# A fused two-layer attention kernel: another way to start the first pass, ffn products in column tiles, and another slot table

## The chip, the cores and the metric

The kernel runs on one core of one Trainium2 chip. The metric is device time in microseconds. The text names the engines as the profile does: PE (matrix products, with PEld for its weight loads), DVE (vector), ACT (activations), POOL, and SP, which only issues transfers.

## The reference, cut to what matters

The input is x, 4 sequences of 1024 tokens with 128 channels. Two layers follow, each an attention and a feed-forward part with a residual and a layernorm behind each. What concerns this case is the first attention and the first feed-forward part:

```python
qkv = einsum('bnc,fc->bnf', x, qkv_w); q, k, v = split(qkv, 3)
q = l2norm(q); k = l2norm(k)             # over all 128 channels of a row
# 16 heads of 8 channels; q and k each times 8**-0.5
attn = softmax(q @ k.T / temperature)    # all 1024 keys
x = layernorm(x + (attn @ v) @ proj_w.T + proj_b)
# ffn of layer 0: int8 product, x quantised row by row
x = layernorm(x + (round(x / scale) @ weight_q.T) * scale * weight_scale + bias)
```

Layer 1 has causal attention with a layernorm and rope on q and k of each head, and a gated silu feed-forward part.

## The kernel before

Tokens are taken in 8 chunks of 512 (`NCH`). One *pass* is one group of 4 heads for 512 queries of one sequence in one layer; there are 64 passes (`PASSES`), taken in pairs. In layer 0 a pass goes over 8 key tiles of 128 keys, in two halves: the first pair of passes takes key tiles 0 to 3 of pass 0, 0 to 3 of pass 1, then 4 to 7 of pass 0 and 4 to 7 of pass 1 (`pair_steps`). A *step* is one key tile (or a packed pair of tiles) for 4 heads. There are 400 steps, and each gives two exps (numbered k = 2s and 2s + 1) of 128x1024, the 800 ACTIVATEs of line 717. For exp k PE makes the scores (`scores`, L874) into one of three PSUM slots, ACT writes `probs`, and PE adds probs times v into bank ACC (`sums`, L896). `scores(k)` waits until exp k - 3 is done.

**Parts and rows.** PE multiplies in a reduced float32 format. To keep precision, q and k are each split into a rounded high part and the rest, the low part (`prep_part`, `mid_part`). A head's 32 rows of `q_st` and `k_st` hold its 8 channels four times (`PRODUCTS`): high and low of q against high and low of k. The rows are laid out by DMA: for most passes through a scratch tensor in DRAM, for pass 0 and the first keys of pass 1 straight from the part tiles (`first_rows`, one DMA for each product y).

**The side work.** All that prepares later passes and finishes earlier ones (qkv products, norms, transposes, layernorms, ffn, gate and up) is cut into units and put between the steps by a table written out beforehand, `ORDER`: one word for each step, whose letters take the next unit of a lane (p: chunk preparation for layer 0, m: middle part, l: last part, c: constants, t: turning the sums). `<` puts the side work ahead of the sums of that slot, `|` puts the sums between the two scores. PE units write the one bank SIDE, DVE reads it, and `side_read` hands it back.

**The head.** Ahead of the steps PE runs 10 dummy bf16 products (`keep_warm`, L930), then the qkv products of chunks 0 and 1 (L938, 128x384 each, into 8 banks). ACT squares q and k of both chunks (L689), copies v and the chunk 1 rows (L703). DVE works out the flags that pick the program's branch, the inverse roots of chunk 0 (9 small operations, L1103 to L271), scales k and q (L1117); PE transposes both (L752); DVE and ACT make the parts (L1332, L1333, L700, L1336). SP and ACT then issue 8 DMAs for pass 0's rows, SP 8 more for pass 1's. PE fills the time with 22 dummy products, takes the branch, and starts `scores`. POOL makes constants; the large memset of `v_st` is behind its first copies.

Of the kernel before, what the change touches and what calls it, by code (L numbers as in the profile page):

```python
# [6 lines left out]
ALU = mybir.AluOpType  # L7
# [132 lines left out]
FIRST_KEYS = [("prep", 1, "pe", "qkT", 1), ("prep", 1, "dve", "scale_q", 0), ("prep", 1, "pe", "qkT", 0)]  # L140
# [17 lines left out]
p p p - - - - <pc < <p - p < <cpp <pp - <t c <p <pp  # L158
- <pc < <p < <p - <p - <ppp < p |t |t |tppmm m - |mmm |p <m
p < mm mmm <mm mmm | |m tm < <m < <m < <mmm - mp <mmm - mp  # L160
m <pm m - |t <tm tm mm <p mm m m pm mmp <mm <mm |m |mmpp |m <
ptm - <m < <m < <m < mmmp <m mp mm pm m p m <tt <m tm <m
<mpm < <mmp <m <mp mmpp <m <mm mmm mp | |m tmp - m - m - <m mm
mm pm - <pm mp < mmp - |t <m tt m m mtp |m <p |mm m <t <mt
tm ll mml <mmm m <m |mml |m pmp m plm mm m <l t <l <mlmm l mp |l
ml ml <m m - l <mp l <l <ll lt <p t <t llmm <pmm mpm - mmp <
lp m m |t <mm mmp <mm <m p m <p <mpp <m <mp <m m <mtt <mm |m |tm
m p <m mp ll <mll m - ll < <l < |tl l l l - |l < l
- l < l < <llll l l |t | |tt mm m <t m mm <mm | |tmm |
|ttl l <lm <m |mm <mml mml m < m m mmm - l t mlm lm ml m |l  # L170
ml ml < <m l l l <ll <l <lm tt < tm <m <m |mm |m |mm |m mm
- |mmlmm | |tmm | |m m < m < m <l <m m m <m |tm | |tmtlm -
<m <ll mm ml < m < ll - <l | <l tl - | |l l l - <l
- <l < <l < <l <ll <l |lltt | |tm mm < t m < <mmm m |ttm |m
<tl <mmm - |mmm |ml |lm lm lm m m ml tlm |l ml lm l l l <mmlm l
<lm m llm < |tt <ml tll < l |t - <llll - l tl tl <tm <lm <mlm <l
<l l <l <lm <llll ml - <lmt <m <m m m m m m m <mm < - mm
mmt
# [95 lines left out]
def program(nc, a, ctx):  # L274
# [11 lines left out]
    w_cols = sb("w_cols", [P, 6 * C + 4], F32)  # L286
    w_qkv = [w_cols[:, 0:3 * C], w_cols[:, 3 * C + 4:6 * C + 4]]
    tcol = w_cols[:, 3 * C:3 * C + 1]
# [51 lines left out]
    job["prep"]["sq"] = job["prep"]["qk"]  # L340
    job["mid"]["sq"] = tok["mid"]["both"][:].rearrange("p a t c -> p (a t c)").rearrange("p (t c) -> p t c", t=TC)
# [16 lines left out]
    head_bank = {1: ps[:, TC, :], 0: ps[:, TC + 1, :]}  # L358
# [13 lines left out]
    more_rows_in, second_rows_in = sem("more_rows_in"), sem("second_rows_in")  # L372
# [9 lines left out]
    tcol_made, head_high = sem("tcol_made"), sem("head_high")  # L382
# [22 lines left out]
    WARM = (10, 4, 0, 22, 7)  # L405
# [15 lines left out]
    def first_rows(eng, p, u, dst, y):  # L421

        part = job["prep"]["part"][p * HR:(p + 1) * HR, u, y % PARTS if u else y // PARTS, :]
        eng.dma_start(dst[y:P:PRODUCTS, p, 0:HALF].bitcast(F32), part.bitcast(F32)).then_inc(rows_in[p], 16)
# [32 lines left out]
    def _(sp):  # L457
# [34 lines left out]
        load_x(1)  # L492
        for dst, src in ((w_qkv[1], a["w1_qkv"]),
# [10 lines left out]
        for u, dst in ((1, k_st), (0, q_st)):  # L504
            sp.wait_ge(parts_ready, 2 - u)
            for y in range(PRODUCTS // 2):
                first_rows(sp, 0, u, dst, y)
        for u, dst in ((1, k_st), (0, q_st)):
            for y in range(PRODUCTS):
                first_rows(sp, 1, u, dst, y)  # L510
# [67 lines left out]
    def _(pool):  # L578
# [67 lines left out]
        send_parts(pool, "prep", 1, 1)  # L646
# [5 lines left out]
        todo = [(s + 1, 0, "mask", s) for s in range(NS) if STEPS[s][3]]  # L652
# [9 lines left out]
        for _, _, what, n in todo:  # L662
            if what == "bias":
                add_bias(n)
            elif what == "mask":
                mask(n)
            elif what == "load":
                load_v(n)
            else:
                store_v(what, n)  # L670
# [3 lines left out]
    def _(act):  # L674
# [4 lines left out]
        def head():  # L679

            act.dma_start(w_cols[:, 0:3 * C + 1], a["w0_qkv"]).then_inc(w_in, 16)
            act.dma_start(small[:], a["small"].partition_broadcast(P)).then_inc(small_in, 16)

            def square(c, t):
                for u in range(2):
                    done = 2 * (c * TC + t) + u
                    if done:
                        act.wait_ge(norms_ready, done)
                    nc.scalar.activation(squares, ps[:, c * TC + t, u * C:(u + 1) * C], ACT.Square,  # L689
# [715 lines left out]
```

## Time and profile before

| | us |
|---|---|
| median of three runs | 810.7 (809.85 to 811.05) |
| the profiled execution | 810.68 |
| its span, first to last instruction | 808.6 |
| PE busy | 791.6 |
| ACT busy | 767.8 |
| DVE busy | 527.7 |
| POOL busy | 174.7 |

Times in views count from the span's start. The profiled execution took 2.08 us more than its span. A busy PE isn't a PE at its peak, since ends of pipelined matmuls are modelled.

### The profile page before, as it was taken

How to read it: one execution, taken by the hardware profiler on the slowest of the kernel's cores; microseconds unless marked ns; L12 is line 12 of the kernel's file. 1: busy time of each engine (PE TensorE's matmuls, PEld its weight loads, DVE VectorE, ACT ScalarE, POOL GpSimd, SP SyncE). 2: the span in 40 equal slices, each digit the busy share in tenths (PEclk: the TensorE clock that was granted, in tenths of full speed). 3: DMA queues.
4: the chain of work that ended last, by engine and by line, in shares of the span. 5: the costliest groups of instructions: out<-in, count | busy, mean ns of one | idle time of the engine just before them, and what ended most of it. 6: DMA issues, size and time to landing. Idle time of an engine off the chain costs nothing.

```text
span 808.6 us, 18428 instructions
## 1 busy us (share of the span) xinstructions
PE 791.6 (98%) x7469; PEld 295.9 (37%) x7469; DVE 527.7 (65%) x1422; ACT 767.8 (95%) x869; POOL 174.7 (22%) x370
## 2 busy tenths in 40 slices
PE   8999999999999999999999999999999999999996
PEld 4333333333333433443333433343333343443444
DVE  4253657758758788687862685766573387787646
ACT  4999999999999999999999999999999999999982
POOL 3111101101102601033100511023300263363220
PEclk9999999999999999999999999999999999999999
DMA  5776232415404711532170431231231231053000
GB/s 148 253 235 208 89 122 82 154 41 183 144 28 157 272 41 40 183 144 93 41 260 27 124 112 42 92 128 44 92 131 51 69 130 54 28 182 120 15 15 16
DMA packets 48553, 88.71 MB, mean 110 GB/s; under 512 B 5200, under 2 KB 14544, under 8 KB 48464
## 3 DMA queue, kind: packets, MB, share of 16 engines
q1 hardware_dynamic: 47696, 85.95, 31.2%
q8 instruction: 61, 1.00, 0.5%
q0 software_dynamic: 288, 1.05, 0.4%
q10 hardware_dynamic: 480, 0.48, 0.2%
q14 instruction: 28, 0.23, 0.1%
HBM read 50.50 MB, written 35.65 MB: 107 GB/s over the span
## 4 chain that ended last, share of the span: by engine, by line
PE 74%; ACT 14%; DVE 7%; issue 3%; POOL 1%; DMA 0%; ACTq 0%; DVEq 0%; POOLq 0%
PE ps L896 36%; PE ps L874 21%; ACT probs L717 13%; PE ps L763 8%; PE ps L752 3%; PE ps L849 2%; DVE th L1282 1%; DVE hT L1283 1%; PE ps L930 1%; PE ps L757 1%; ACT th L677 0%; PE ps L938 0%; DVE gate_sb L1279 0%; POOL v_all L590 0%; PE ps L791 0%
## 5 line engine op out<-in xcount | busy, mean ns | idle before, releaser
L717 ACT ACTIVATE probs<-ps 128x1024 f32<-128x1024 f32 x800 | 745.9, 1057 | 15.3 <-PE ps L874 11.3
L896 PE MATMUL ps<-probs,v_st 128*32 128x512 f32 (+3 forms) x3584 | 425.0, 556 | 3.3 <-issue 1.8
L874 PE MATMUL ps<-q_st,k_st 32*128 32x512 f32 (+3 forms) x1792 | 257.4, 459 | 2.1 <-ACT probs L717 0.9
L874 PEld LDWEIGHTS ps<-q_st,k_st 32*128 32x128 f32 x1792 | 119.6, 182 | 281.8 <-ACT probs L717 226.5
L627 POOL TENSOR_SCALAR_AFFINE_SELECT probs<-probs 128x256 f32<-128x256 f32 x256 | 104.3, 430 | 141.0 <-ACT probs L717 138.9
L896 PEld LDWEIGHTS ps<-probs,v_st 128*32 128x32 f32 x3584 | 79.9, 108 | 110.2 <-issue 80.9
L595 POOL COPY v_st<-v_all 128x256 f32<-128x256 f32 (+1 forms) x65 | 25.6, 402 | 343.3 <-PE ps L896 335.2
L1256 DVE COPY mid_qkv<-ps 128x384 f32<-128x384 f32 x32 | 17.8, 558 | 45.5 <-PE ps L763 43.8
L1137 DVE STREAM_TRANSPOSE sums_t<-ps 128x512 f32<-128x512 f32 x32 | 22.9, 717 | 29.1 <-PE ps L896 29.0
L1287 DVE TENSOR_TENSOR last_y<-ps,last_y 128x128 f32<-128x128 f32 x24 | 7.0, 292 | 42.6 <-PE ps L763 42.6
L849 PE MATMUL ps<-yTp,w_hid 128*128 128x512 f32 x84 | 30.8, 448 | 1.7 <-DVE gate_sb L1279 0.3
L1256 DVE COPY prep_qkv<-ps 128x384 f32<-128x384 f32 x24 | 13.4, 557 | 27.4 <-PE ps L763 27.0
L590 POOL COPY v_all<-mid_qkv 128x512 f32<-128x512 f32 x9 | 14.0, 1552 | 66.4 <-DVE mid_qkv L1256 61.5
L763 PE MATMUL ps<-w_cols,yT 128*32 128x384 f32 x256 | 26.8, 491 | 0.0
L763 PE MATMUL ps<-w_down,hT 128*32 128x128 f32 x672 | 23.9, 275 | 0.6 <-DVE last_y L1287 0.3
L1233 DVE TENSOR_TENSOR x_all<-ps,x_all 128x512 f32<-128x512 f32 x15 | 10.4, 692 | 20.5 <-PE ps L763 19.3
L1282 DVE SCALAR_TENSOR_TENSOR th<-th,gate_sb 128x512 f32<-128x512 f32 x21 | 14.7, 698 | 13.5 <-PE ps L849 10.8
L1279 DVE COPY gate_sb<-ps 128x512 f32<-128x512 f32 x21 | 14.5, 691 | 13.1 <-PE ps L849 12.8
L763 PEld LDWEIGHTS ps<-w_down,hT 128*32 128x32 f32 x672 | 17.9, 110 | 12.2 <-issue 6.8
L849 PEld LDWEIGHTS ps<-yTp,w_hid 128*128 128x128 f32 x84 | 12.5, 188 | 24.8 <-DVE gate_sb L1279 10.3
L617 POOL TENSOR_TENSOR x_all<-x_all,vecs 128x512 f32<-128x512 f32 x16 | 20.4, 1278 | 0.6 <-DMA x_all<-in_x 0.6
L763 PE MATMUL ps<-w_cols,xT 128*32 128x384 f32 x192 | 20.2, 492 | 0.0
(192 smaller groups left out, 636.2 us busy)
## 6 DMA issues: line engine op xcount, KB each, us to landing
k_st<-parts_scratch SPq DMA_DIRECT2D x46, 512.0 KB, 3.5
parts_scratch<-mid_part SPq DMA_DIRECT2D x34, 512.0 KB, 4.0
q_st<-parts_scratch SPq DMA_DIRECT2D x62, 256.0 KB, 3.9
parts_scratch<-prep_part SPq DMA_DIRECT2D x28, 512.0 KB, 4.3
k_st<-parts_scratch SPq DMA_DIRECT2D x17, 256.0 KB, 2.8
xT<-in_xT SPq DMA_DIRECT2D x8, 256.0 KB, 4.2
x_all<-in_x SPq DMA_DIRECT2D x8, 256.0 KB, 6.6
out<-yo SPq DMA_DIRECT2D x7, 256.0 KB, 2.3
```

The costliest lines, as they stand in the source:

```text
L595: return g_.tensor_copy(v_st[:, p % VB, t, :, p % 2 * SR:p % 2 * SR + D], v_all[:, layer, b % 2, t, g * GH * D:(g + 1) * GH * D] .rearrang ...
L617: g_.tensor_tensor(x_all[:, c, :, :], x_all[:, c, :, :], bc(vecs[:, 3 * layer, :].unsqueeze(1), [P, TC, C]), ALU.add).then_inc(bias_added, 1)
L627: op = g_.affine_select(out=block_, in_=block_, compare_op=ALU.is_ge, fill=0.0, base=0, pattern=[[0, 2], [1, P]], channel_multiplier=-1)
L717: nc.scalar.activation(probs[:, k % PS, :, 0:w], slot(k)[:, :, 0:w], ACT.Exp).then_inc(probs_ready, 1)
L752: last_ = tp(dst[:, t * P:(t + 1) * P], src(t), idn[:])
L763: last_ = mm(dst[row, :], src[:, row], w, start=first, stop=last)
L849: last_ = mm(side, w_hid[:, 0 if what == "gate" else 1, k * P:(k + 1) * P], yTp[:, n, :], start=(n == 0), stop=(n == PARTS - 1))
L874: last_ = mm(slot(k)[:, e, at:at + n], k_st[row, p % KB, kt * P:(kt + 1) * P], q_st[row, p % KB, lo:HALF], start=True, stop=not shifted)
L896: last_ = mm(acc[HR * h:HR * (h + 1), lo:HALF], v_st[:, p % VB, kt, h, :], probs[:, (2 * s + h // 2) % PS, h % 2, at:at + n], start=FIRST[ ...
L1137: v.transpose(sums_t[:], acc).then_inc(sums_turned, 1)
L1256: v.tensor_copy(job[name]["qkv"][:, k, :], side[:, 0:3 * C]).then_inc(side_read, 1)
L1282: chain[lane(name, c)].link(stt(out=th[:, k % 2, :], in0=th[:, k % 2, :], scalar=1.0, in1=gate_sb[:, k % 2, :], op0=ALU.add, op1=ALU.mult))
```

## The change

- **Pass 0's rows in place.** Chunk 0's products are made as q, k and v groups of 4 products of 128x128 in banks ACC, SIDE and 5. DVE takes k's squares with `bn_stats`. It writes the scaled q and k of the first 4 heads with every channel four times over (`first_qk`), so that PE's transpose gives all 128 rows at once. ACT writes them times +1 or -1 by row, rounded, and DVE adds the unrounded rows times 0 or 1, which gives high or low part by row. No DMA is in this. The second keys of pass 0 come the same way from chunk 1, as a unit `firstT` in slot 3.
- **The usual parts of chunk 0** (`head_turn`) are made behind the first three `scores`. SP and POOL then load the rows of pass 1, each DMA as soon as its part is there, and SP stores the parts to DRAM right behind; sums of step 0 wait for these parts. The DRAM load of pass 1's second keys is replaced by 4 DMAs from the part tile. Four DMAs that ACT issued are gone, and four of pass 0's second keys.
- **Dummy products**: 8 instead of 10, then 3, then 8 (instead of 4 and 22), and two each behind scores 4, 5 and 7 instead of scores 3 to 6.
- **POOL** does its memsets ahead of the v copies; its store of chunk 1's k parts moves into its list.
- **SP** holds the 9 loads of later constants until x's first chunk has landed.
- **ffn**: four products of 32 output columns in place of each 128x128 one.
- **ORDER** is another table. The same units, plus `firstT` and `scale_k`, in the same order within each lane.

```diff
-FIRST_KEYS = [("prep", 1, "pe", "qkT", 1), ("prep", 1, "dve", "scale_q", 0), ("prep", 1, "pe", "qkT", 0)]
+FIRST_KEYS = [("prep", 1, "pe", "firstT", 1), ("prep", 1, "dve", "scale_k", 0), ("prep", 1, "pe", "qkT", 1), ("prep", 1, "dve", "scale_q", 0), ("prep", 1, "pe", "qkT", 0)]
...
-p p p - - - - <pc < <p - p < <cpp <pp - <t c <p <pp
...
+- - | <pc ppc p p - <p p < <p - <pp <p <p <tp p < p
...
-    WARM = (10, 4, 0, 22, 7)
+    HEAD_SQUARES = 2
+    WARM = (8, 3, 8, (4, 5, 7))
...
+        eng.dma_start(dst[y:P:PRODUCTS, p, 0:HALF].bitcast(F32), part.bitcast(F32)).then_inc(done or rows_in[p], 16)
...
+        sp.wait_ge(x_in[0], 16)
...
+            for low in range(PARTS - u):
+                sp.wait_ge(*((parts_ready, 2 - u) if low else (head_high, 2 - u)))
+                for y in range(PRODUCTS):
+                    if (y % PARTS if u else y // PARTS) == low:
+                        first_rows(sp, 1, u, dst, y)
+        store_parts("prep", 0, 1)
+        store_parts("prep", 0, 0)
...
+            sp.dma_start(k_st[y:P:PRODUCTS, 1, HALF:S].bitcast(F32),
+                         job["mid"]["part"][HR:2 * HR, 1, y % PARTS, :].bitcast(F32)).then_inc(second_rows_in, 16)
...
+        pool.wait_ge(qkv_copied, 1)
+        pool.sem_inc(v_stored["prep"], 1)
+        pool.wait_ge(pool_consts, POOL_CONSTS + 1)
+        copy_v(0, slice(0, TC)).then_inc(v_in, 1)
+        store_v("prep", 1)
+        pool.wait_ge(v_stored["prep"], 2)
+        copy_v(0, slice(TC, KT)).then_inc(more_v_in, 1)
+        pool.wait_ge(parts_ready, 1)
+        for y in range(1, PRODUCTS, PARTS):
+            first_rows(pool, 1, 1, k_st, y, low_rows_in)
...
+        todo = [(slot_of("prep", 1, "qkT", 1) + 1, 0, "send", 1)] + [(s + 1, 0, "mask", s) for s in range(NS) if STEPS[s][3]]
...
+                send_parts(pool, "prep", n, 1)
...
+            act.wait_ge(head_qkv, 1)
             for t in range(TC):
-                act.wait_ge(head_qkv, t + 1)
...
+                square(t, ps[:, ACC, t * P:(t + 1) * P], job["prep"]["st"][:, 0, 2 * t:2 * t + 1])
+            act.wait_ge(head_qkv, 3)
+            nc.scalar.activation(v_all[:, 0, 0, tiles_of(0), :], ps[:, V_BANK, :].rearrange("p (t c) -> p t c", t=TC),
+                                 ACT.Copy).then_inc(qkv_copied, 1)
...
-                if t == TC - 1:
+                act.wait_ge(head_qkv, 4 + t)
+                for u in range(2 if t < HEAD_SQUARES else 0):
+                    square(TC + 2 * t + u, ps[:, t, u * C:(u + 1) * C], job["mid"]["st"][:, 0, 2 * t + u:2 * t + u + 1])
+                if t == HEAD_SQUARES:
...
+                    for u in (1, 0):
+                        act.wait_ge(first_turned, 2 - u)
+                        nc.scalar.activation(first_sign[:, u, :], ps[:, FIRST_BANK[u], :], ACT.Copy,
+                                             scale=(sign_q, sign_k)[u]).then_inc(first_signed, 1)
+                nc.scalar.activation(job["mid"]["qkv"][:, t, :], ps[:, t, 0:3 * C], ACT.Copy).then_inc(
+                    qkv_copied if t == TC - 1 else head_copied, 1)
...
-                pe.wait_ge(side_read, fill)
+            pe.wait_ge(*((side_read, fill) if fill else (parts_ready, 2)))
...
-                    last_ = mm(side[:, t * P:(t + 1) * P], xqT[:, t * P:(t + 1) * P], w_ffn[:], start=True, stop=True)
+                    last_ = quarters(side[:, t * P:(t + 1) * P], xqT[:, t * P:(t + 1) * P], w_ffn[:])
...
+            elif what == "firstT":
+                pe.wait_ge(first_scaled, 3)
+                last_ = turn4(lambda t: first_qk[:, t, k, :, :].rearrange("p f y -> p (f y)"), side, ident)
...
-                    pe.wait_ge(rows_in[p % KB], 32 * (p // KB + 1) + (32 * PRODUCTS - 32 if p % KB < 2 else 0))
+                    pe.wait_ge(*((first_made, 2) if not p else (rows_in[p % KB], 32 * (p // KB + 1) + {0: -32, 1: 32 * PRODUCTS - 64}.get(p % KB, 0))))
+                    if p == 1:
+                        pe.wait_ge(low_rows_in, 16 * PARTS)
...
-                pe.wait_ge(more_rows_in, 16 * PRODUCTS)
+                pe.wait_ge(side_read, FILL["prep", 1, "firstT", 1] + 1)
             if k % 2 == 0 and tiles_[0][0:2] == (1, TC):
-                pe.wait_ge(second_rows_in, 16)
+                pe.wait_ge(second_rows_in, 16 * PRODUCTS)
...
+                pe.wait_ge(parts_ready, 2)
...
-        keep_warm(WARM[0], SIDE)
+        keep_warm(WARM[0], 0)
...
+        pe.wait_ge(x_in[0], 16)
+        for n, bank in enumerate((ACC, SIDE, V_BANK)):
             for t in range(TC):
-                mm(ps[:, c * TC + t, 0:3 * C], xT[:, c, t * P:(t + 1) * P], w_qkv[0],
-                   start=True, stop=True).then_inc(head_qkv, 1)
+                last_ = mm(ps[:, bank, t * P:(t + 1) * P], xT[:, 0, t * P:(t + 1) * P], w_qkv[0][:, n * C:(n + 1) * C],
+                           start=True, stop=True)
+            last_.then_inc(head_qkv, 1)
+        pe.wait_ge(x_in[1], 16)
+        for t in range(TC):
+            mm(ps[:, t, 0:3 * C], xT[:, 1, t * P:(t + 1) * P], w_qkv[0], start=True, stop=True).then_inc(head_qkv, 1)
+        keep_warm(WARM[1], FIRST_BANK[1])
...
+        pe.wait_ge(qkv_copied, 1)
...
+            pe.wait_ge(first_scaled, 2 - u)
+            for t in range(TC):
+                last_ = tp(ps[:, FIRST_BANK[u], t * P:(t + 1) * P], first_qk[:, t, u, :, :].rearrange("p f y -> p (f y)"), ident[:])
+            last_.then_inc(first_turned, 1)
+        pe.wait_ge(head_copied, 1)
+        keep_warm(WARM[2], 0)
...
+        pe.wait_ge(qkv_copied, 2)
...
+        def head_turn(u):
+            pe.wait_ge(qk_ready["prep"], 2 - u)
+            turn4(lambda t: job["prep"]["qk"][:, t, u * C:(u + 1) * C], ps[:, ACC + u, :], ident).then_inc(head_turned, 1)
...
+                head_turn(1)
+                head_turn(0)
...
+                    if k in WARM[3]:
+                        pe.wait_ge(parts_ready, 1)
+                        keep_warm(2, SIDE)
...
-                        keep_warm(2, ACC)
...
+            if not part:
+                ch.step(v.tensor_reduce(m[:, 0:1], temp, AX.X, ALU.max, apply_absolute_value=True))
+                ch.step(v.tensor_reduce(m[:, 2:4], gb[:, 0, :, :], AX.X, ALU.max, apply_absolute_value=True))
+                return
+            ch.need()
+            ch.step(ts(far[:, 0:1], m[:, 0:1], BOUND * D, None, ALU.is_gt))
...
+            elif what == "firstT":
+                chain[name].link(ts(first_sign[:, k, :], side, sign_k, None, ALU.mult))
+                stt(out=k_st[:, 0, HALF:S], in0=side, scalar=low_k, in1=first_sign[:, k, :].bitcast(F32),
+                    op0=ALU.mult, op1=ALU.add).then_inc(side_read, 1)
...
+        def head():
+            ch, part, qk = chain["prep"], job["prep"]["part"], job["prep"]["qk"]
+            per = lambda c, k: buffers("prep", c)["st"][:, k, 0:2 * TC].rearrange("p (t u) -> p t u", u=2)
+            by_t = lambda x: x.rearrange("p (t c) -> p t c", t=TC)
+            roots = lambda c: [rows_norm("prep", c, what) for what in ("rs1", "rs2")]
+            dve.wait_ge(head_qkv, 2)
+            bn, mv, mean2 = tok["last"]["bn"], tok["last"]["st"][:, 0, :], tok["last"]["st"][:, 1, 0:TC]
+            mean, var = mv[:, 0:2 * TC:2], mv[:, 1:2 * TC:2]
+            for t in range(TC):
+                ch.step(v.bn_stats(bn[:, t, :], by_t(side)[:, t, :]))
+            ch.need()
+            for t in range(TC):
+                ch.step(v.bn_aggr(mv[:, 2 * t:2 * t + 2], bn[:, t, :]))
+            ch.need()
+            ch.link(stt(out=mean2, in0=mean, scalar=float(C), in1=mean, op0=ALU.mult, op1=ALU.mult))
+            ch.link(stt(out=per(0, 0)[:, :, 1], in0=var, scalar=float(C), in1=mean2, op0=ALU.mult, op1=ALU.add))
+            dve.wait_ge(norms_ready, TC)
+            roots(0)
+            for u in (1, 0):
+                op = tt(first_qk[:, :, u, :, :], by_t(ps[:, ACC + u, :])[:, :, 0:HR].unsqueeze(3).to_broadcast([P, TC, HR, PRODUCTS]),
+                        per(0, 1)[:, :, u].unsqueeze(2).unsqueeze(3).to_broadcast([P, TC, HR, PRODUCTS]), ALU.mult)
+                op.then_inc(first_scaled, 1)
+            flags(1)
+            for u, dst in ((1, k_st[:, 0, 0:HALF]), (0, q_st[:, 0, :])):
+                dve.wait_ge(first_signed, 2 - u)
+                stt(out=dst, in0=ps[:, FIRST_BANK[u], :], scalar=(low_q, low_k)[u], in1=first_sign[:, u, :].bitcast(F32),
+                    op0=ALU.mult, op1=ALU.add).then_inc(first_made, 1)
+            for u in (1, 0):
+                tt(qk[:, :, u * C:(u + 1) * C], by_t(ps[:, ACC + u, :]), bc(per(0, 1)[:, :, u].unsqueeze(2), [P, TC, C]),
+                   ALU.mult).then_inc(qk_ready["prep"], 1)
+            dve.wait_ge(head_turned, 1)
+            v.tensor_copy(part[:, 1, 0, :], side).then_inc(head_high, 1)
+            dve.wait_ge(head_high, 1)
+            tt(part[:, 1, 1, :], side, part[:, 1, 0, :].bitcast(F32), ALU.subtract).then_inc(parts_ready, 1)
+            dve.wait_ge(head_turned, 2)
+            ts(part[:, 0, 0, :], acc, tcol, None, ALU.mult).then_inc(head_high, 1)
+            dve.wait_ge(head_high, 2)
+            stt(out=part[:, 0, 1, :], in0=acc, scalar=tcol, in1=part[:, 0, 0, :].bitcast(F32), op0=ALU.mult,
+                op1=ALU.subtract).then_inc(parts_ready, 1)
+            dve.wait_ge(qkv_copied, 2)
+            late = slice(HEAD_SQUARES, TC)
+            wide = lambda x: x.rearrange("p t (u c) -> p t u c", u=2)
+            rest = job["mid"]["sq"][:, late, :]
+            ch.link(tt(rest, job["mid"]["qkv"][:, late, 0:2 * C], job["mid"]["qkv"][:, late, 0:2 * C], ALU.mult))
+            ch.link(v.tensor_reduce(per(1, 0)[:, late, :], wide(rest), AX.X, ALU.add))
+            dve.wait_ge(norms_ready, TC + 2 * HEAD_SQUARES)
+            roots(1)
+            tt(first_qk[:, :, 1, :, :], job["mid"]["qkv"][:, :, C:C + HR].unsqueeze(3).to_broadcast([P, TC, HR, PRODUCTS]),
+               per(1, 1)[:, :, 1].unsqueeze(2).unsqueeze(3).to_broadcast([P, TC, HR, PRODUCTS]), ALU.mult).then_inc(first_scaled, 1)
...
+        flags(0)
+        head()
...
+def low_and_sign():
+    y = np.arange(P) % PRODUCTS
+    low = np.stack([y // PARTS, y % PARTS]).astype(np.float32)
+    return np.stack([low[0], 1 - 2 * low[0], low[1], 1 - 2 * low[1]], axis=1)
```

## Rows read from the trace of the kernel before

**Rows 1.** The page: busy time by engine, and the chain that ended last

```profile
PE 791.6 (98%) x7469; PEld 295.9 (37%) x7469; DVE 527.7 (65%) x1422; ACT 767.8 (95%) x869; POOL 174.7 (22%) x370
...
PE 74%; ACT 14%; DVE 7%; issue 3%; POOL 1%; DMA 0%; ACTq 0%; DVEq 0%; POOLq 0%
```

**Rows 2.** Timeline of ACT, 19 to 790 us: start, length, count, idle before

```profile
19.83 126.84 ACT L717 ACTIVATE probs<-ps 128x1024 f32<-128x1024 f32 x137 [4.08 <-PE ps L874]
```

**Rows 3.** Waits of ACT, 40 to 784 us: total, times, longest

```profile
ACT probs L717 <- PE ps L874: 7.2, 27, 0.6
```

**Rows 4.** Timeline of all engines, 0 to 14 us

```profile
1.27 4.45 PE L930 MATMUL ps<-warm 128*128 128x512 bf16 x10 [1.27 <-DVE warm L997]
...
5.08 0.77 PEld L938 LDWEIGHTS ps<-w_cols,xT 128*128 128x128 f32 x2 [0.28 <-DMA w_cols<-in_w_qkv]
...
5.51 5.63 PE L938 MATMUL ps<-w_cols,xT 128*128 128x384 f32 x16
...
10.04 0.17 DVE L1103 TENSOR_SCALAR prep_st<-prep_st 128x8 f32<-128x8 f32 x1 [1.55 <-ACT attn L689]
...
11.05 0.48 ACT L703 ACTIVATE mid_qkv<-ps 128x384 f32<-128x384 f32 x1
...
11.87 1.29 DVE L1117 TENSOR_TENSOR prep_qk<-ps,prep_st 128x512 f32<-128x512 f32 x2
...
12.61 1.32 PE L752 MATMUL ps<-ident,prep_qk 128*128 128x128 f32 x8
```

**Rows 5.** Timeline of all engines, 14 to 32 us (a merged row may start earlier)

```profile
13.76 4.91 PE L930 MATMUL ps<-warm 128*128 128x512 bf16 x22
...
14.03 0.69 ACT L700 ACTIVATE prep_part<-ps,w_cols 128x512 fp32r<-128x512 f32 x1 [0.42 <-PE ps L752]
...
14.88 0.75 DVE L1336 SCALAR_TENSOR_TENSOR prep_part<-ps,w_cols,prep_part 128x512 fp32r<-128x512 f32 x1 [0.16 <-DVE prep_part L1333]
...
19.30 0.73 PE L874 MATMUL ps<-q_st,k_st 32*128 32x512 f32 x6 [0.63 <-DMA q_st<-prep_part]
...
19.83 13.19 ACT L717 ACTIVATE probs<-ps 128x1024 f32<-128x1024 f32 x14 [4.08 <-PE ps L874]
...
19.88 2.51 SPq L424 DMA_DIRECT2D q_st<-prep_part  x4
```

**Rows 6.** Line 938 alone, 0 to 12 us: ns min/median/max

```profile
L938 PEld LDWEIGHTS ps<-w_cols,xT x16: 190/190/338, 5.1 to 10.3; 128*128 128x128 f32 x16
L938 PE MATMUL ps<-w_cols,xT x16: 485/487/794, 5.5 to 10.7; 128*128 128x384 f32 x16
```

**Rows 7.** Timeline of the kernel's end: small f32 products, bn_stats and bn_aggr

```profile
786.92 1.16 PE L777 MATMUL ps<-x_all,ident 128*128 128x128 f32 x8
...
789.74 0.97 DVE L1190 BATCH_NORM_STATS2 last_bn<-ps 128x6 f32<-128x128 f32 x4 [0.32 <-PE ps L783]
...
790.75 0.38 DVE L1065 BATCH_NORM_AGGREGATE last_tok<-last_bn 128x2 f32<-128x6 f32 x4
```

**Rows 8.** The DMAs of line 424, from issue to landing

```profile
DMA to landing us min/median/max: 2.1/2.1/2.3
```

**Rows 9.** Line 449: how long POOL takes to issue a DMA, ns

```profile
L449 POOL DMA_DIRECT2D parts_scratch<-mid_part x2: 786/793/800, 22.4 to 23.1; - x2
```

**Rows 10.** DMA issues: POOL's two, KB each, us to landing

```profile
parts_scratch<-mid_part POOLq DMA_DIRECT2D x2, 512.0 KB, 4.2
```

**Rows 11.** Pieces of the chain that ended last: start, us, count

```profile
101.78 0.99 PE ps L896 x8
102.78 0.33 PE ps L838 x4
...
106.45 0.43 PE ps L874 x2
...
585.86 1.08 PE ps L763 x32
```

**Rows 12.** Line 838 alone, the ffn weight load: ns min/median/max

```profile
L838 PEld LDWEIGHTS ps<-w_ffn,xqT x32: 96/98/100, 102.7 to 666.5; 128*128 128x128 bf16 x32
```

More of the change, by code:

```diff
@@ L176 @@
-<lm m llm < |tt <ml tll < l |t - <llll - l tl tl <tm <lm <mlm <l
-<l l <l <lm <llll ml - <lmt <m <m m m m m m m <mm < - mm
-mmt
+- - | <pc ppc p p - <p p < <p - <pp <p <p <tp p < p
+c <p - pc < <p - p - p - <ppp |t |pt |tm < <mp |mm |mmp -
+<mmp < <mm <m mmm <m |mm |m tm - <m - m - m m < <mmp <mmmm <pm
+m p < <m ttm - tm <mm <pm - - - <m |mpmmm mpm - |mmmm |mmp |pm -
+ptm < <m - <m - <mm <mm pm m p <mm p <mm p m t <m tt mmmm
+p mm <p - <m <mpm <mpp |mmm <m |m | |mmpm ptm - m < <m - <mm <mm
+<mpm < < <pmm pm m <p - |tt <m t m mm tp | <mp <m m mtmt -
@@ L179 @@
+< <l - <l - <lll <lll < |t |t |t <m <mm <t <m <mm < |m |mtm |tm
+<tl <mmm <m |mm | |mllm lm m lm mm l |tl ml ml l ml lm lm lm l
+<l lmm lm < |lt <mt tl < |ll <t lll < |l |l tl tl <tm <lm <ml <ml
+<l l <l ml <lll lm l <lmt <m <m m m m m <m <m <m <m <mmmm |
+t
 """
@@ L284, in program @@
     v_all = sb("v_all", [P, 2, 2, KT, C], F32)
-    w_cols = sb("w_cols", [P, 6 * C + 4], F32)
-    w_qkv = [w_cols[:, 0:3 * C], w_cols[:, 3 * C + 4:6 * C + 4]]
-    tcol = w_cols[:, 3 * C:3 * C + 1]
+    w_cols = sb("w_cols", [P, 6 * C + 8], F32)
+    w_qkv = [w_cols[:, 0:3 * C], w_cols[:, 3 * C + 8:6 * C + 8]]
+    tcol, first_tcol = w_cols[:, 3 * C:3 * C + 1], w_cols[:, 3 * C + 1:3 * C + 2]
+    low_q, sign_q, low_k, sign_k = [w_cols[:, 3 * C + n:3 * C + n + 1] for n in range(2, 6)]
     w_out = sb("w_out", [P, 2, C], F32)
@@ L666, in _ @@
                 mask(n)
+            elif what == "send":
+                send_parts(pool, "prep", n, 1)
             elif what == "load":
@@ L679, in head, with square @@
         def head():
-            act.dma_start(w_cols[:, 0:3 * C + 1], a["w0_qkv"]).then_inc(w_in, 16)
+            act.dma_start(w_cols[:, 0:3 * C + 6], a["w0_qkv"]).then_inc(w_in, 16)
             act.dma_start(small[:], a["small"].partition_broadcast(P)).then_inc(small_in, 16)
[L684 to L689, printed above, removed]
-                                         accum_out=buffers("prep", c)["st"][:, 0, 2 * t + u:2 * t + u + 1]).then_inc(norms_ready, 1)
+            def square(n, src, sums_):
+                if n:
+                    act.wait_ge(norms_ready, n)
+                nc.scalar.activation(squares, src, ACT.Square, accum_out=sums_).then_inc(norms_ready, 1)
@@ L887, in sums @@
                         pe.wait_ge(sums_turned, p // 2)
+            if not s:
+                pe.wait_ge(parts_ready, 2)
             if tiles_[0][0:2] == (0, TC):
@@ L962, in steps @@
             if not shifted:
-                stage("prep", 1, "qkT", 1)
+                head_turn(1)
+                head_turn(0)
             for s in range(NS + 1):
@@ L974, in steps @@
                 for name, c, e, what, k in SIDE_ORDER[s]:
-                    if e == "pe" and (name, c, e, what, k) != FIRST_KEYS[0] and \
-                            not (shifted and (name, c, e, what, k) in FIRST_KEYS):
+                    if e == "pe" and not (shifted and (name, c, e, what, k) in FIRST_KEYS):
                         stage(name, c, what, k)
```

128 lines of the change are left out of this document (30 added, 98 removed).

## The prediction

> **What bounds the kernel now.** I read the page first. PE is busy 98% of the span and ACT 95%, and the chain that ended last is PE 74% and ACT 14% [rows 1]: two engines in lockstep, neither with room to spare. The timeline of ACT alone shows which of them leads. The first exp starts at 19.83 us, and 137 exps then run without a gap that is listed, 0.926 us apart (126.84 / 137) [rows 2]. In this stretch ACT sets the pace, so whatever brings the first exp forward brings all of it forward, as long as PE can feed it. Later ACT waits for scores: 7.2 us in 27 waits between 40 and 784 us, the longest 0.6 [rows 3], where PE's side work is the bound. After the last exp the end is a chain of its own, which the change leaves alone.
>
> So there are three questions: when does the first exp start, does the start lose anything again in the first eight steps, and what do table and ffn do to the 7.2 us.
>
> **When the first exp starts.** Before, the ways to it are: dummies to 5.71 (they start at 1.27 and last 4.45), products, ACT's squares until DVE's first root operation at 10.04, nine root operations until 11.87, scaling, transposes at 12.61 [rows 4], parts until 15.6 (14.88 + 0.75), then DMAs, whose landing ends PE's wait at 19.30, and the exp at 19.83, 0.53 later [rows 5]. From the parts to the exp that is 4.2 us, of which 2.1 are the flight of the last DMA [rows 8]. After:
>
> 1. Two dummies fewer. The weight load waited for the landing at 5.08 and the product started at 5.51 behind the dummies [rows 4]. Now the product follows the load: 5.08 + 0.338 = 5.42 [rows 6]. The two fewer dummies are worth only 0.1, because data bound it as well.
> 2. Three groups of 4 small float32 products. The like-sized L777 took 1.16 for its 8 instructions with the last one's tail, so 0.136 each and 1.09 a group [rows 7]. The first L938 instructions ran at the low clock (load 338 ns against 190, product 794 against 487) [rows 6]; I add 0.3 for two or three such loads. q is done at about 7.0, k at 8.1, v at 9.2, then chunk 1 at 0.35 each (5.63 / 16, two instructions a product [rows 4]), last at 11.85.
> 3. DVE on k: four bn_stats 0.97 and four bn_aggr 0.38 [rows 7], then two linked small operations at 0.2 ((11.87 - 10.04) / 9 [rows 4]): 8.1 to 9.95. ACT squares q meanwhile: four, even at half a microsecond each, from 7.0 to 9.0, so it is hidden; cover left 0.9.
> 4. Nine root operations, 1.83: 11.8. Spread k, then q, 0.65 each (two in 1.29 [rows 4]): 12.45 and 13.1.
> 5. Six flag operations at 0.2, which before stood ahead of the wait for ACT and cost nothing: to 14.3. Beside them PE transposes k (0.66, half of 1.32 [rows 4]) to 13.15 and q to 13.85, and ACT writes the signed rows, 0.69 each [rows 5]: 13.9 and 14.6. DVE's flags are the later one for k.
> 6. DVE's two sums of rows at 0.75 (L1336 [rows 5]): 15.05 and 15.85.
> 7. PE's dummies don't hold it up: 8 at 0.22 (4.91 / 22 [rows 5]) end at 15.65. Nor do ACT's last two copies, 0.48 each from 14.6 [rows 4], end 15.6. These three lie within 0.3 us, so there is no cover: any of them late is late one for one. What the branch itself costs is not visible; between the end of the dummies (13.76 + 4.91 = 18.67) and the scores at 19.30 there was 0.63, so at most that. Behind 15.65 it would give 16.25 instead of 15.9; I take it as hidden, since PE's queue runs ahead of its products, and keep 0.35 for the range.
> 8. Scores at 15.9, exp 0.53 later: **16.45**, against 19.83. The gain is 3.4.
>
> **What the first steps give back.** Pass 1's rows are needed by exp 8, due at 16.45 + 8 x 0.926 = 23.86. DVE now makes the parts after the rows: scales k and q to 17.15, then, once PE has transposed (0.66 behind the first scores, 17.25), k's parts at 0.69 each (18.65) and q's at 0.75 each (20.2). SP issues a DMA every 0.63 (2.51 / 4 [rows 5]): k's two from 17.95, q's high two from 19.4, q's low two from 20.7, the last issued at 21.3 and landed at 23.4 [rows 8]. POOL issues its two in 1.6 from 18.65 [rows 9]; its transfers of 512 KB landed in 4.2 [rows 10], so these of 64 KB by 23.7 at worst, 21.6 at SP's flight time. Scores at 23.5 give exp 8 at 24.05: **0.2** lost. Behind it are queued on PE sums of step 1 to 3 and `firstT`, on SP the four stores to DRAM. `firstT` waits for DVE: behind 20.2 come squares and their sum 1.4, roots 1.83, spreading 0.65, so 24.1, just when PE gets there. With it and `qkT` (0.66 each) slots 3 and 4 carry 0.99 of sums, 0.43 of scores [rows 11] and 0.66, 2.1 of PE work for 1.85 of exps. By my sum scores 11 and 13 are ready 0.2 to 0.3 ahead of need; a small error turns that into a wait, so between 0 and 1.2 are lost, and I take 0.1 more. Net of the start: 3.4 - 0.3 = **3.1**. POOL's memsets, now ahead of the v copies, are hidden by its wait for the first v: POOL is busy 22% of the time [rows 1]. Without that cover each microsecond of them would delay v and the sums of step 0. SP's late loads feed the constants of a later slot; were they late, DVE would stand at its first constant unit.
>
> **ffn.** Eight times, 4 products took 0.33 on the chain. In quarters there are 16 of each instruction; the 32 instructions of `proj` took 1.08, that is 0.034 each, and each streams float32, so the bf16 ones take between 0.21 (four quarters at once, the arithmetic of 128 columns scaled from 0.22 per 512) and 0.54 [rows 5, 11]. The saving of a switch between wide and narrow loads lies within the same 0.1 to 0.2. Eight times that is -1.0 to +1.7, and most ffns lie where ACT leads. I take 0. The Trainium skill (TensorEngine Tiling (Array Packing), Restrictions) says that column tiling turns the fast weight load off. The wide load took 98 ns for 128 columns [rows 12]; no row shows a narrow bf16 one. By that rule the upper end would hold, and the time would be the rival below.
>
> **The table.** I compared the words slot by slot: about 40% of the units move, nearly all by one or two slots, either way, and every turn stays put. The sum of PE work is the same. It moves the 27 waits but hardly their sum: 0, with 1.5 either way as a bound, a fifth of the 7.2.
>
> **Sum.** 810.68 (own span 808.6 and 2.08 around it) - 3.1 = **807.6**. The profiled execution is at the median of the runs (810.7), so nothing is to be corrected.
>
> **Rivals.**
> - *The table helps too* (0.12): the units lie more evenly, and a fifth to two thirds of the 7.2 goes: 802.8 to 806.2, likelier near the upper end. For it speaks only that there are waits.
> - *The start gives all back* (0.08): pass 1's rows or `firstT` come 3 us late, since DVE, SP and POOL do in series behind the first scores what was done ahead of them. That the change in effect doesn't do what it says: the first exp at 16.5, but exp 8 or 13 at its old time: 810.5. Against it: the times above leave only tenths.
> - *ffn dearer* (0.06): all eight on the path at +0.21: 807.6 + 1.7 = 809.3. For it: 16 loads in place of 4. Against it: 137 exps in a row show no wait [rows 2], so an ffn among them is hidden. The Trainium skill's rule (TensorEngine Tiling (Array Packing), Restrictions) is this case.
> - *The table costs* (0.08 for 1.5 to 4.5 us, 809.1 to 812.1; 0.05 beyond): units in groups (`mmmm`, `|mmmm`, `firstT` early) hold PE when ACT needs scores. It ends on the slower side once the waits grow from 7.2 by more than 4.7, two thirds more: 812.3 and above, say 813.
> - *The clock* (0.03): PE's dummies now end at 4.7 and it idles until 5.1. The first products ran low before too [rows 6]. If the clock stayed low through q's and k's groups, each would cost 8 x 0.148 = 1.2 more in loads, 2.4 together, and all of chunk 1 another 8 x 0.307 = 2.5 in products: 812.5. It eats the gain up once 3.1 are lost, that is when it lasts into chunk 1, and ends as slower only if nearly all of it is paid.
>
> **How the numbers follow.** My own case holds 0.58, with a range of its own from 806.2 (start's full 3.4, branch hidden, 1 from the table) to 809.0 (branch 0.35, start 1.0 more). Faster or slower counts from 0.2%, 1.6 us, about what a measurement of this kernel can tell from no change: 809.1 and 812.3. Faster: 0.58 + 0.12 = 0.70. Same: 0.08 + 0.06 + 0.08 = 0.22. Slower: 0.05 + 0.03 = 0.08. The range reaches from 805.2, leaving half of the helping table out, to 810.6, leaving out half of the table's cost and the slower ones.
>
> **What would show it.** First exp between 16.2 and 17.0; `first_made` behind ACT's signed rows and the flags, no DMA ahead of the first scores; ACT's wait at exp 8 under 0.5; PE's loads at 190 ns by the second group; ACT's waits after 40 us within 5.7 to 8.7; ffn groups at 0.2 to 0.5. The prediction is wrong if the first exp is later than 17.5, if ACT waits more than 1.5 between exps 3 and 16, or if the waits after 40 us change by over 2.

## The result and the profile after

The change made the kernel slower: 814.56 us median of 6 runs (814.01 to 815.65) against 810.54 of 6 (809.85 to 811.05), ratio 1.0048 with a 95% interval of 1.0038 to 1.0059. I had forecast 807.6. The profiled execution took 814.01, its span is 812.3, against 810.68 and 808.6.

The page of the changed kernel, busy time and chain, looks like [rows 1]. It doesn't say what went wrong:

```profile
PE 789.7 (97%) x7574; PEld 296.1 (36%) x7574; DVE 535.0 (66%) x1443; ACT 766.5 (94%) x854; POOL 175.7 (22%) x372
...
PE 76%; ACT 10%; DVE 9%; issue 4%; POOL 1%; DMA 0%; SPq 0%; DVEq 0%; ACTq 0%; POOLq 0%
```

The timeline of ACT does, where one row of 137 exps stood before [rows 2]:

```profile
14.77 7.44 ACT L723 ACTIVATE probs<-ps 128x1024 f32<-128x1024 f32 x8 [0.75 <-PE ps L884]
23.04 13.94 ACT L723 ACTIVATE probs<-ps 128x1024 f32<-128x1024 f32 x15 [0.83 <-PE ps L884]
42.52 1.94 ACT L723 ACTIVATE probs<-ps 128x1024 f32<-128x1024 f32 x2 [5.55 <-PE ps L884]
45.12 1.94 ACT L723 ACTIVATE probs<-ps 128x1024 f32<-128x1024 f32 x2 [0.66 <-PE ps L884]
47.27 101.61 ACT L723 ACTIVATE probs<-ps 128x1024 f32<-128x1024 f32 x110 [0.21 <-PE ps L884]
...
786.37 2.86 ACT L723 ACTIVATE probs<-ps 128x1024 f32<-128x1024 f32 x3 [0.15 <-PE ps L884]
```

The first exp starts 5.06 us sooner than before. Exp 8 waits 0.83, and then there is one wait of 5.55 behind exp 22. The last row of exps before was this one:

```profile
782.88 2.86 ACT L717 ACTIVATE probs<-ps 128x1024 f32<-128x1024 f32 x3 [0.20 <-PE ps L874]
```

From such rows I cut every execution into four stretches: to the first exp; from its start until the first 137 are done; from there until all 800 are done; and from there to the end of the span.

| execution | first exp | 137 exps | the other 663 | end | span |
|---|---|---|---|---|---|
| before | 19.83 | 126.84 | 639.07 | 22.86 | 808.6 |
| after | 14.77 | 134.11 | 640.35 | 23.07 | 812.3 |
| difference | -5.06 | +7.27 | +1.28 | +0.21 | +3.7 |

So the change gains 5.1, loses 7.3 among the first 137 exps and 1.3 behind them. The waits of ACT beyond 50 us, 7.8 in 25, are close to [rows 3].

The chain through the long wait names its cause. Columns: start, length, what:

```profile
30.91 0.76 DVE mid_part L1303
...
31.70 0.75 DVE mid_part L1304
32.45 0.54 DVEq L1406
...
33.34 0.07 DVEq L1419
33.42 4.35 issue
37.76 0.23 DVE w_ffn L1058
37.99 0.47 DVE w_hid L1059
38.46 0.27 DVE w_down L1060
...
39.65 0.56 DVE prep_qkv L1283
40.21 0.04 issue
40.25 1.51 PE ps L769 x8
41.76 0.73 PE ps L884 x3
42.49 1.87 PE ps L908 x8
```

L1406 is DVE's load of the flag, L1419 its branch, `with dve.If(far_scores > 0): steps(True)`, and `Else: steps(False)` behind it. With this data the flag is 0, so DVE jumps over all the code of the shifted steps, and nothing is issued for 4.35 us. Everything from L1058 on is code behind the jump. The constants' six units take 1.9 and then DVE copies the qkv product out of bank SIDE (L1283), for which PE has waited 4.3 us. The waits of that stretch, total, times, longest:

```profile
DVE w_ffn L1058 <- issue: 5.3, 1, 5.3
...
PE ps L769 <- DVE prep_qkv L1283: 4.3, 1, 4.3
```

PE's idle time has an echo. Windows by 2 us; after the five engines comes the granted clock, then the DMA share and GB/s:

```profile
36.00:38.00 2.00, 0.00 (x0) 0.00 (x0) 0.24 (x2) 0.97 (x2) 0.00 (x0) 1.00 0.49 172
38.00:40.00 2.00, 0.00 (x0) 0.00 (x0) 1.93 (x6) 0.00 (x0) 0.00 (x0) 0.60 0.04 12
40.00:42.00 2.00, 1.75 (x12) 0.49 (x12) 0.37 (x2) 0.00 (x0) 0.00 (x0) 0.50 0.90 295
42.00:44.00 2.00, 2.00 (x12) 0.20 (x8) 0.38 (x1) 1.48 (x2) 0.00 (x0) 0.50 0.81 238
44.00:46.00 2.00, 2.00 (x20) 0.73 (x20) 0.00 (x0) 1.34 (x2) 0.00 (x0) 0.69 0.96 300
46.00:48.00 2.00, 2.00 (x20) 0.35 (x12) 0.56 (x1) 1.79 (x3) 0.00 (x0) 1.00 0.98 367
```

PE had no work from 35.99 to 40.25. The granted clock averages 0.60 from 38 to 40 us and is at the lower of the two levels, 0.50 or 1.2 GHz, from 40 to 44. Eight sums take 1.87 in the chain instead of 0.99 [rows 11]; from 46 us on the clock is at 2.4 GHz again.

The jump was there before the change too. DVE in the kernel before:

```profile
28.69 0.75 DVE L1273 SCALAR_TENSOR_TENSOR mid_part<-ps,w_cols,mid_part 128x512 fp32r<-128x512 f32 x1
36.27 0.56 DVE L1256 COPY prep_qkv<-ps 128x384 f32<-128x384 f32 x1 [6.83 <-PE ps L763]
```

Its last work ahead of the branch ended at 29.44, and its next was due at 36.27, waited for by nobody until PE had made the product. The jump must lie in the 6.8 us between; that trace doesn't show how long it is, and the second experiment below tests what it cost. In the changed kernel DVE's work ahead of the branch ends at 32.45, 3 us later although the first exp is 5 sooner: `scale_k` and `firstT` are now ahead of it, and the usual parts of chunk 0 are made behind the first scores. The new table also puts the constants (`pc ppc`) ahead of the first copy.

### The profile page after: what moved, and what is told of

It is laid out like the page before. It is cut to its first block, busy times and chain, and to the rows that moved or that the text cites. A ratio compares the mean times of both kernels' runs of the same rounds, so it can differ in the third digit from the quotient of the medians.

```text
span 812.3 us, 18629 instructions
## 1 busy us (share of the span) xinstructions
PE 789.7 (97%) x7574; PEld 296.1 (36%) x7574; DVE 535.0 (66%) x1443; ACT 766.5 (94%) x854; POOL 175.7 (22%) x372
## 4 chain that ended last, share of the span: by engine, by line
PE 76%; ACT 10%; DVE 9%; issue 4%; POOL 1%; DMA 0%; SPq 0%; DVEq 0%; ACTq 0%; POOLq 0%
PE ps L908 37%; PE ps L884 22%; PE ps L769 9%; ACT probs L723 9%; PE ps L758 4%; PE ps L857 2%; DVE th L1313 1%; DVE hT L1314 1%; PE ps L763 1%; ACT th L685 0%; DVE gate_sb L1310 0%; PE ps L942 0%; POOL v_all L594 0%; PE ps L797 0%; DMA q_st<-prep_part 0%
## 5 line engine op out<-in xcount | busy, mean ns | idle before, releaser
L1283 DVE COPY mid_qkv<-ps 128x384 f32<-128x384 f32 x32 | 17.8, 558 | 47.5 <-PE ps L769 46.8
L1283 DVE COPY prep_qkv<-ps 128x384 f32<-128x384 f32 x24 | 13.3, 556 | 21.3 <-PE ps L769 20.9
```

Of the source, the lines that this page charges most:

```text
L1283: v.tensor_copy(job[name]["qkv"][:, k, :], side[:, 0:3 * C]).then_inc(side_read, 1)
```

## The experiments

The kernels ran in three groups, in which the kernel before had medians of 810.60, 810.57 and 810.66, so times can be compared across groups. Labels name them: "turned" means VectorE's branch turned, unless SyncE's is named.

**VectorE's branch turned.** Only the order of the two bodies in the code is swapped, so the path that runs falls through.

```diff
-        with dve.If(far_scores > 0):
-            steps(True)
+        with dve.If(far_scores < 1):
+            steps(False)
...
         with dve.Else():
-            steps(False)
+            steps(True)
```

> The changed kernel with one edit: DVE's branch is written the other way round, so that the path taken follows it directly, as PE's already does; before, DVE jumped over the whole other path. Theory J (the jump): in the changed kernel DVE did nothing from its branch at 33.4 us to 37.76, then was behind by its constants, PE waited 4.3 for its copy and ACT 5.55, and PE's clock fell to 1.2 GHz. Without the jump DVE's next instruction follows the branch within 0.5 us, ACT's waits of 5.55, 0.66 and 0.21 near 42 us are gone or under 1 together, the clock stays at 2.4 GHz, and the time is 814.6 - 6 = 808 to 809. Rival L (DVE is late by its own work: firstT, scaling and parts end 3.0 us later after the branch's place than before, and then come constants): the idle of 4.35 stays or is only shared out, and the time stays within 1 of 814.6. Rival F (the code has to be fetched on either path): the gap stays near 4.4 and so does the time.

Measured: 808.45 (808.01 to 809.42, 10 runs), ratio to before 0.9974 (0.9965 to 0.9984). That is 6.1 less than the changed kernel, from this swap alone. ACT's timeline, and DVE's first unit behind the branch:

```profile
15.93 7.44 ACT L723 ACTIVATE probs<-ps 128x1024 f32<-128x1024 f32 x8 [0.75 <-PE ps L884]
24.14 13.93 ACT L723 ACTIVATE probs<-ps 128x1024 f32<-128x1024 f32 x15 [0.77 <-PE ps L884]
38.31 105.33 ACT L723 ACTIVATE probs<-ps 128x1024 f32<-128x1024 f32 x114 [0.24 <-PE ps L884]
```

```profile
34.50 0.23 DVE L1058 CAST w_ffn<-w_ffn 128x128 bf16<-128x128 int8 x1 [0.96 <-issue]
```

DVE stands for 0.96 instead of 5.3, ACT's wait of 5.55 has become 0.24, and the clock stays at 1.00 in the windows from 34 to 44 us. Taken from the first exp, DVE's copy L1283 comes at 20.46 instead of 24.88, so 4.4 of the gain are the jump. ACT's stretch of 137 exps is 6.4 shorter (127.71 against 134.11). The other 2.0 are what PE lost behind the stop. The low clock accounts for about as much, as an estimate: the first three pieces behind the stop took 1.51, 0.73 and 1.87 in the changed kernel's chain, and the same kinds of piece take 0.78, 0.44 and 0.99 in this one's, 1.9 less together. No run separates it.

The stop isn't a draw of one execution. In the three other kernels with the new head and VectorE's branch as it was (ffn as before, the old table from slot 14, and SyncE's branch turned, all below), the same piece behind L1419 took 4.42, 4.35 and 4.26 us.

**The same swap in the kernel before.**

> The kernel before with the same turn of DVE's branch. There DVE stood still from 29.98 to 34.5 as well, but its next work came from PE only at 36.27. Theory J: the stop was hidden, so the time stays within 0.5 of 810.6; if it is 2 or more faster, the stop cost something before too.

Measured: 810.52 (809.95 to 811.22, 10 runs), ratio 0.9999 (0.9989 to 1.0009). The jump cost nothing before, as the traces said: DVE stands for 6.82 ahead of the same copy, against 6.83, with the jump or without it. Together the two runs show that the change laid bare a stop that was hidden.

**ffn as before, in the changed kernel.**

```diff
-                    last_ = quarters(side[:, t * P:(t + 1) * P], xqT[:, t * P:(t + 1) * P], w_ffn[:])
+                    last_ = mm(side[:, t * P:(t + 1) * P], xqT[:, t * P:(t + 1) * P], w_ffn[:], start=True, stop=True)
```

> The changed kernel with the ffn's four products of 128 columns as before. If the column tiles are dearer, as the prediction's rival had it, this is up to 1.7 us faster than 814.6; theory J says that they have nothing to do with the loss, and expects it within 0.7 of 814.6, with each ffn back at 0.33 on the chain.

Measured: 814.99 (814.39 to 815.60, 4 runs), ratio 1.0053 (1.0035 to 1.0071): no difference from the changed kernel. The 663 exps took 640.36 against 640.35. In the chain of the changed kernel an ffn in quarters costs what the four wide products cost [rows 11]:

```profile
104.14 0.34 PE ps L769 x16
```

**The old table from slot 14 on, in the changed kernel.**

> The changed kernel with the slot table of before from slot 14 on (the first 14 words stay the new ones, since the new head needs its two more units there). Rival T (the new table costs): ACT's waits after 50 us fall from 7.9 to 7.2 or below and the time by 1 or more. Theory J: the stretch up to 47 us is as in the changed kernel, all of the loss stays, the time is within 1 of 814.6.

Measured: 814.18 (813.54 to 814.92, 5 runs), ratio 1.0047 (1.0032 to 1.0062). By the time alone the table looks neutral, and the stop is still there, 5.58. The stretches tell more: the 663 exps took 639.24, 1.1 less than with the new table, and the first 137 took 134.72, 0.6 more, of which 0.2 is the wait at exp 8 (1.06 against 0.83). It looked like two effects that cancel within what the time can show; so I tried both tables where the stop is gone.

**The branch turned, with the old table from slot 14 and from slot 68.**

> The changed kernel with VectorE's branch turned (so that the two-sided code without the shift falls through), and the old slot table from slot 14 on. Theory T (the new table costs): from exp 137 to the last exp the trace has 639.07 us with the old table (before), 640.35 with the new one (changed kernel and the one with the branch turned), 639.24 with the old table in the changed kernel, so about 1.1 comes back; up to exp 137 the old table took about 0.4 more. Expected 807.6 to 808.0 us, 0.7 under the 808.45 of the turned branch with the new table, and 639.2 from exp 137 to the end. Theory N (the table is neutral, as my prediction had it): 808.45 within 0.3.

> The changed kernel with VectorE's branch turned, the new table up to slot 67 and the old one from slot 68 on. Theory T: the new table is better by 0.4 up to exp 137 and dearer by 1.1 behind it, so this is the fastest of the tables: 807.2 to 807.5 us. Theory N (the table is neutral): 808.45 within 0.3.

Measured: 807.76 (806.86 to 808.44, 5 runs), ratio 0.9965 (0.9952 to 0.9979), and 807.19 (807.02 to 808.17, 5 runs), ratio 0.9961 (0.9948 to 0.9975). The 663 exps took 639.02 and 639.37. Against 808.45 with the new table throughout, the new one costs about 1 us behind slot 68. That it gains in the first part isn't shown: the first 137 took 127.97 and 128.13, no less than the 127.71 with the new table all through, and the two medians differ by less than their intervals.

**The new table from slot 68 in the kernel before.**

> The kernel before with the new slot table from slot 68 on, and nothing else of the change. Theory T (the new table costs 1.1 to 1.3 behind exp 137 whatever stands ahead of it): 811.6 to 811.9 us, and 640.2 to 640.4 from exp 137 to the last one instead of 639.07. Theory N (it cost that only in the changed kernel, by its later slots meeting other work): 810.6 within 0.3.

Measured: 811.60 (810.93 to 812.40, 11 runs), ratio 1.0015 (1.0006 to 1.0024), the lower end of what was expected. The first 137 exps are at 126.84 as before, the 663 at 640.11. The table costs 1.0 by itself, whatever the head is. All profiled executions agree: the 663 exps took 639.02 to 639.60 in the seven kernels with the old table behind slot 68, and 640.11 to 640.38 in the seven with the new one. Which slots cost it stays open.

**The last of pass 1's q rows by POOL.** The stretch of 137 exps is still 0.9 longer than before, nearly all of it the wait at exp 8.

```diff
+        pool.wait_ge(parts_ready, 2)
+        first_rows(pool, 1, 0, q_st, 3, low_rows_in)
```

(and SP leaves y = 3 out; the counts that PE and DVE wait for follow)

> The changed kernel with VectorE's branch turned, and the last of pass 1's four query stores (y = 3) issued on GpSimd's queue instead of SyncE's. Theory Q (exp 8 waits for SyncE's sixth store in a row, issued 0.6 us apiece): the wait of 0.77 before exp 8 falls to 0.2 to 0.4, and the time from 808.45 to 807.9 to 808.1. Theory P (the wait is for the rows of the low part itself, or GpSimd's queue lands as much later as SyncE's was busy): the wait stays over 0.6, the time within 0.3 of 808.45.

Measured: 808.76 (808.29 to 809.49, 10 runs), ratio 0.9978 (0.9968 to 0.9987): nothing gained. The wait is 0.73. In the second try POOL issues a row whose part is ready earlier, so that SP's last two start sooner:

> VectorE's branch turned, the old table from slot 68 on, and pass 1's query store y = 1, of the high part, issued on GpSimd's queue behind its two key stores. SyncE's last two stores then start about 0.6 us sooner, since the part they carry is ready from 18.5 on. Theory Q (exp 8 waits for SyncE's last store): the wait before exp 8 falls from 0.8 to 0.3 and the time from 807.2 to about 806.7. Theory P (the row by GpSimd's queue lands last, as y = 3 did at 23.0): the wait stays over 0.5, the time within 0.3 of 807.2.

Measured: 807.83 (807.54 to 809.32, 6 runs), ratio 0.9971 (0.9959 to 0.9983), the wait 0.91. Not faster either. The lines of these DMAs, first the changed kernel, then this one:

```profile
DMA to landing us min/median/max: 2.1/2.5/3.0
```

```profile
L430 POOL DMA_DIRECT2D q_st<-prep_part x1: 540/540/540, 19.4 to 19.4; - x1
...
DMA to landing us min/median/max: 2.1/2.5/3.5
```

POOL's issue starts at 19.4, behind its two k rows, and the slowest landing takes 0.5 longer. That slowest one isn't POOL's row, which took 2.9 here and 3.4 in the first try: in the chains of both tries PE waits for the last row of SP's own queue, for 3.5 us from its issue, against 3.0 in the changed kernel. So what SP's queue saves, the flight loses, and theory P was right about the wait but not about the queue. In [rows 8] such transfers took 2.1 to 2.3.

**Without SP's wait for the first tokens.**

```diff
-        sp.wait_ge(x_in[0], 16)
```

> The changed kernel with VectorE's branch turned, and without SyncE's wait for the first tokens ahead of its late loads. Theory H (the hold lets the query, key and value weights land 0.2 to 0.5 us sooner): the first product stands 0.2 to 0.5 later and the time is 808.6 to 809.0. Rival: the weights are the first transfer issued on ScalarE's queue and land as soon either way: 808.45 within 0.2.

Measured: 808.69 (807.76 to 809.77, 8 runs), ratio 0.9978 (0.9967 to 0.9988). The first product starts at 4.87 against 4.91 with the wait. Holding the late loads back has no effect that the time shows.

**SyncE's branch turned.** SP jumps over the same kind of body (33.9 to 39.15 without a transfer issued in the changed kernel), so it had to be told apart from DVE's.

```diff
-        with sp.If(far_scores > 0):
-            steps(True)
-        with sp.Else():
-            steps(False)
+        with sp.If(far_scores < 1):
+            steps(False)
+        with sp.Else():
+            steps(True)
```

> The changed kernel with SyncE's branch turned and VectorE's left as it is. SyncE stops for about 5 us behind its own jump too, so it is the rival for the stop: its k_st load for the next pass was late. Theory D (VectorE's jump alone costs): 814.6 within 0.4, and ScalarE's wait of 5.5 stays at its place. Theory S (SyncE's stop costs too): 810 to 813.

> The changed kernel with VectorE's and SyncE's branches turned, and the old table from slot 68 on. Theory D: SyncE's stop is hidden even when VectorE's is gone: 807.2 within 0.4, the time with VectorE's branch alone turned. Theory S: 806 to 806.8.

Measured: 816.64 (816.07 to 817.62, 5 runs), ratio 1.0077 (1.0063 to 1.0091), 2.1 slower than the changed kernel; and 809.20 (808.54 to 809.87, 11 runs), ratio 0.9984 (0.9975 to 0.9993), 2.0 slower than 807.19. Neither theory expected a loss. ACT's 5.43 stayed where it was in the first of them, so the stop that matters in the start is DVE's. SP's jump was hidden there by something else: turned, SP stands in the same place for its own stores of the parts to land (`DMA parts_scratch<-mid_part`, 3.2 and 2.6 us in the two runs), and its next transfer starts only 0.9 and 1.1 us sooner, counted from the first exp.

The loss is at the other side: the end, behind the last exp, takes 24.53 and 24.88 instead of 23.07 and 22.96 in the kernels they are compared with (22.86 to 23.40 in all the others). SP's waits beyond 790 us, in the kernel with DVE turned (old table from slot 68) and in the one with both turned:

```profile
SPq L491 <- DVE yo L1245: 19.1, 1, 19.1
SPq L1475 <- DMA out<-yo: 1.3, 1, 1.3
```

```profile
SPq L491 <- DVE yo L1245: 19.1, 1, 19.1
SPq L1475 <- PEq L1475: 0.2, 1, 0.2
```

Normally SP stands for 1.3 us until the last store has landed. Turned, it doesn't: when it arrives, the store has landed already. Its last issue began at 803.4 and landings took at most 2.4 from there, so the store was down by 805.8, while the span ends at 807.8. The body that falls through is now followed by the `Else` body, which SP has to jump over before its last wait. No row shows that jump itself, but in both runs the order of the bodies is all that differs. So the jump isn't gone, it has moved to the exit, and there SP has nothing to hide it under but one landing. DVE has nothing behind its bodies, so its exit jump is free (the end took 22.91 with DVE alone turned).

## Why the prediction was wrong, step by step

**The step that failed** is "What the first steps give back". It followed rows, parts and sums, and it named the place: "were they late, DVE would stand at its first constant unit". But it looked only for late loads there. In step 7 I priced the branch for PE alone (0.63 at most), and for DVE and SP not at all, although the change moved the work around DVE's branch. What the runs showed in its place: 4.35 us without issue behind L1419 plus the low clock behind it, 6.4 us of the 137 exps, gone when the branch was turned. None of the rivals had this mechanism. By its number 814.56 lies nearest to the dearest form of "The table costs" (812.3 and above, 0.05), but the table cost only 1.0 to 1.3; nor did pass 1's rows or `firstT` come 3 us late, and the clock fell behind the stop and not in the head. Of my signs that the forecast would fail, a wait over 1.5 between exps 3 and 16 was set too early; it came behind exp 22. The last one did fire, though for the stop and not for the table it was meant for: from 40 us on ACT waits 14.2 instead of 7.2.

**Exp 8** waited 0.8, not 0.2. The mechanism was right (SP's queue, then the flight); the flight was 2.1 to 3.0 and not 2.1, with eight of these transfers issued within 4 us.

**First exp (steps 1 to 8).** Mechanism right, gain mis-sized: forecast 16.45, measured 14.77. The changed kernel:

```profile
4.72 2.92 PE L950 MATMUL ps<-w_cols,xT 128*128 128x128 f32 x24
...
11.24 1.17 PE L962 MATMUL ps<-ident,prep_qkv 128*128 128x128 f32 x8 [0.37 <-DVE prep_qkv L1371]
...
14.22 0.73 PE L884 MATMUL ps<-q_st,k_st 32*128 32x512 f32 x6
```

Of the 1.7, 1.3 were there when k was done: DVE's bn_stats began at 6.78 and not 8.1, because the product started 0.7 sooner than step 1 has it, a group took 0.97 instead of 1.09 and the slow first loads of step 2 didn't come (no load of L950 took more than 192 ns; with the branch turned the longest took 333). Step 2 put such loads down to the low clock. The kernel before has 1.00 for the granted clock in the window from 5 to 6 us, where its load of 338 ns lies, so that column doesn't show it, and what slows them stays open. Two sums there are slightly off: step 3's terms end at 9.85 and not at 9.95, which made the forecast 0.1 later, and chunk 1 ends nearer 12.0 than 11.85, on which nothing rests. From there the nine roots, flags and rows took what was forecast within 0.4. But one profile is a draw: the first exp lay between 14.77 and 15.93 in eleven executions of the new head, median 15.40, and at 18.92, 19.64 and 19.83 in three of the old. Median against median the head is worth 4.2, not the 5.1 of the two first profiles and not the 3.4 forecast.

**ffn at 0** holds. The rule that column tiling turns the fast weight load off (the Trainium skill, TensorEngine Tiling (Array Packing), Restrictions) shows in no time here. A narrow load took 92 to 97 ns for a quarter of the columns, a wide one 96 to 100 [rows 12], so by the column the narrow one isn't faster, and no run tells whether that is the rule or a fixed cost. But the whole group took 0.34 against 0.33, and the upper end that I had tied to the rule didn't come.

**The table at 0** was off by about 1.0 to 1.3, inside the 1.5 kept as a bound. The waits I meant to judge it by moved only from 7.2 to 7.8 and 25 for 27; gaps too small to be listed aren't in that sum. The stretch of 663 exps showed it at once.

The sum made good, in the profiled executions: -5.06 (first exp) +0.8 (exp 8) +6.4 (stop and clock) +1.3 (table) +0.2 (end and rest) = +3.7, the difference of the spans. With DVE's branch turned and the old table behind slot 68 the change comes to 807.19, near the 807.6 that I had forecast for it as it was. That nearness is partly luck: the head is worth 4.2 and not 3.4, and the first 137 exps are 1.3 longer than before (128.13 against 126.84), where I had given back 0.3. That version, the changed kernel with DVE's branch turned and the old table from slot 68, beats both kernels.

## What to carry to other kernels

When work around a branch moves, price the branch on every engine that takes it, and not only on the one that leads: find in the trace the engine's last row ahead of it and its first behind it, and ask who waits for that second row. Put the body that runs for your data where the engine falls through, but look at what stands behind the bodies, since the jump then comes at the exit. And compare an edit by a stretch between two fixed instructions, where a microsecond is visible that the total time and the listed waits don't show.

## What the hardware did that I had not expected

- A jump over a long body stopped DVE for 4.35 us; falling through into the same code, flag load included, cost 0.96. What in the jump takes the time, no row shows. With SP's bodies swapped, so that the jump lies at its exit, the end of the kernel was 1.5 to 1.9 us longer.
- The first float32 products of the head run at different speeds from one execution to the next at a granted clock of 1.00 throughout: 24 instructions of L950 took 2.92 in the changed kernel and 3.89 in the one with the branch turned, with identical code up to there. This is most of the difference between the first exps of these two, 14.77 and 15.93.
- Issuing one of SP's six small row transfers from POOL's queue freed its place in SP's line, but the slowest landing went from 3.0 to 3.5, and it was still SP's own last one.
